# DLRM tower with a CIN: the first transfers in another order, a shorter tail of the program, and x_pair read from two copies

## The reference, cut to what matters

```python
e = jnp.stack([tbl_f[ids[:, f]] for f in range(32)], axis=1)      # 512 x 32 x 16
x0 = h = e
for i in range(3):                                                # W_i: 128 x (32 * G), G = 32, 64, 64
    z = (x0[:, :, None, :] * h[:, None, :, :]).reshape(B, F * G, E)
    y = relu(einsum('oc,bce->boe', W_i, z) + b_i)                 # 128 channels
    x_keep, h = (y[:, :64], y[:, 64:]) if i < 2 else (y, y)
    xs.append(x_keep)
z = sum(concat(xs, axis=1), axis=2)                               # 512 x 256
h = concat([z, dense_ctx], axis=1)                                # 512 x 272
h = maximum(h @ W_top1 + b_top1, 0); h = maximum(h @ W_top2 + b_top2, 0); y = h @ W_top3
```

## Time and profile before

| | |
|---|---|
| median of 3 runs | 548.99 us (548.51 to 549.04) |
| the profiled execution's own time | 548.4 us |
| its span, first to last instruction | 546.6 us |
| mean granted TensorE clock | 0.978 of full |
| PE busy | 505.7 us, 93% |
| DVE, ACT, POOL busy | 376.5, 198.8, 364.1 us |
| moved by DMA | 94.49 MB, mean 173 GB/s |

### The profile page before, as it was taken

The page is one execution under the profiler, slowest core; times in us unless marked ns, Lnnn a source line. Parts: engine busy times, 40 slices in busy tenths (PEclk is TensorE's granted clock), DMA queues, the critical chain, the costliest instruction groups (busy, mean ns, idle before and its releaser), DMA issues.

```text
span 546.6 us, 4327 instructions
## 1 busy us (share of the span) xinstructions
PE 505.7 (93%) x1474; PEld 277.4 (51%) x1474; DVE 376.5 (69%) x216; ACT 198.8 (36%) x257; POOL 364.1 (67%) x222
## 2 busy tenths in 40 slices
PE   0977947899999999999999999999999989899988
PEld 0733414455555555565555555555555554455555
DVE  1274526595959595959688695959595968967743
ACT  1212132433444443424342434434443525241244
POOL 5770527497969788796969696969697754715050
PEclk9988887899999999999999999999999999999999
DMA  7697989349997979797878787979789777451200
GB/s 229 144 201 204 210 221 196 100 98 252 222 251 170 255 159 254 158 227 166 230 164 226 172 215 165 225 167 244 164 197 222 171 190 161 90 110 11 74 0 0
DMA packets 33591, 94.49 MB, mean 173 GB/s; under 512 B 7889, under 2 KB 15057, under 8 KB 25122
## 3 DMA queue, kind: packets, MB, share of 16 engines
q1 hardware_dynamic: 27090, 90.82, 69.5%
q10 hardware_dynamic: 2384, 2.35, 2.0%
q0 software_dynamic: 4096, 1.06, 1.6%
HBM read 92.04 MB, written 2.10 MB: 172 GB/s over the span
## 4 chain that ended last, share of the span: by engine, by line
PE 73%; DMA 8%; DVE 7%; issue 4%; POOL 3%; SPq 2%; ACT 1%; POOLq 1%; DVEq 0%; ACTq 0%
PE acc L605 26%; PE acc L618 14%; PE spare L605 12%; PE x_bank L605 11%; DMA x_scratch<-gathered 4%; DVE z L414 4%; PE x_bank L618 3%; PE spare L618 3%; POOL gathered L349 3%; DMA gathered<-in_table,rows_all 2%; DMA x_rot<-x_scratch 1%; SPq L276 1%; POOLq L146 1%; DVE zl_parts L426 1%; PE acc L628 1%
## 5 line engine op out<-in xcount | busy, mean ns | idle before, releaser
L362 POOL TENSOR_TENSOR z_low<-z,z_high 128x1024 fp32r<-128x1024 f32 x90 | 221.4, 2472 | 130.1 <-ACT z_high L498 129.4
L414 DVE TENSOR_TENSOR z<-h,x_pair 128x2048 f32<-128x2048 f32 (+1 forms) x65 | 144.8, 2249 | 106.1 <-ACT h L512 104.6
L605 PE MATMUL acc<-z,w_direct 128*128 128x512 f32 x384 | 176.3, 603 | 15.2 <-DVE z L414 15.2
L349 POOL DMA_INDIRECT gathered<-in_table,rows_all x128 | 142.5, 1113 | 33.4 <-issue 27.1
L498 ACT ACTIVATE z_high<-z 128x1024 fp32r<-128x1024 f32 x90 | 93.3, 1054 | 145.1 <-DVE z L414 124.9
L605 PEld LDWEIGHTS acc<-z,w_direct 128*128 128x128 f32 x384 | 73.6, 193 | 95.7 <-issue 72.6
L605 PE MATMUL spare<-z,w_direct 128*128 128x512 f32 x200 | 92.4, 603 | 4.5 <-DVE z L414 4.5
L605 PE MATMUL x_bank<-z,w_direct 128*128 128x512 f32 x200 | 92.5, 608 | 3.9 <-DVE z L414 3.9
L414 DVE TENSOR_TENSOR z<-h_odd,x_pair 128x2048 f32<-128x2048 f32 x32 | 72.2, 2278 | 8.4 <-ACT h_odd L512 8.4
L414 DVE TENSOR_TENSOR z<-h_even,x_pair 128x2048 f32<-128x2048 f32 x32 | 72.2, 2279 | 7.9 <-ACT h_even L512 7.9
L605 PEld LDWEIGHTS spare<-z,w_direct 128*128 128x128 f32 x200 | 38.4, 193 | 47.9 <-issue 43.0
(11 more groups left out here) (140 smaller groups left out, 266.4 us busy)
## 6 DMA issues: line engine op xcount, KB each, us to landing
x_pair<-x_scratch SPq DMA_DIRECT2D x124, 512.0 KB, 7.3
x_rot<-x_scratch SPq DMA_DIRECT2D x60, 256.0 KB
x_rep<-x_scratch SPq DMA_DIRECT2D x15, 256.0 KB
w_direct<-in_W SPq DMA_DIRECT2D x2, 1024.0 KB, 8.5
gathered<-in_table,rows_all POOLq DMA_INDIRECT x128, 7.1
x_scratch<-gathered SPq DMA_DIRECT2D x32, 64.0 KB, 1.6
x_pair<-x_scratch ACTq DMA_DIRECT2D x4, 512.0 KB, 16.5
x_pair<-in_W_top SPq DMA_DIRECT2D x2, 512.0 KB, 4.7
```

What stands on the lines that cost most here:

```text
L349: pool.indirect_dma_start(gathered[:, c % X_SLOTS, j, :], None, table, bass.IndirectOffsetOnAxis(ap=rows.bitcast(U32), axis=0),).then_inc( ...
L362: nc.gpsimd.tensor_tensor(z_low[:, slot_of(pair)], products_of(pair), z_high[:, slot_of(pair)].bitcast(F32), ALU.subtract).then_inc(low_po ...
L414: nc.vector.tensor_tensor(z[:, step.group % Z_SLOTS, first:end], h[:].unsqueeze(1).to_broadcast([P, end - first, N]), x_pair[:, chunk % 2, ...
L605: op = nc.tensor.matmul(bank_of(pair)[:], w_direct[:, first + i], products_of(pair)[:, i], start=i == 0 and pair is OPENS[pair.layer, pair ...
```

## The change: what it does

- BUSY is 28 instead of 56.
- The x_pair loads of chunk 0: parts 0 and 1 from both queues, then the store of chunk 1, then parts 2 and 3 from SP. After that x0 of chunk 1, the store of chunk 2, parts 0 and 1 of chunk 1, then a wait for the product (0, 1, 0) and the squares of chunk 1, x0 of chunk 2, parts 2 and 3 of chunk 1. The loop leaves out what was moved.
- FIRST has (2, 0, 1) ahead of (0, 1, 0), and the split pairs of (0, 1) are due one step behind their product, not two. The product of (2, 0, 0) is made in two halves, as that of (1, 0, 0) was, with a signal after each.
- The split pairs of layer 2, chunk 15 get their low part from VectorE, one step after the product (LOWS).
- Top layers: the bias of the first one is a 17th row of the dense weights against a column of ones (K = 51); ACT makes the rounded ReLU in one pass; VectorE takes max(bank, 0) less the rounded part; the second layer's matmuls with the high part wait for ACT alone.
- load_half: of the 64 partitions of a half, even ones read the first copy of the rows in x_scratch and odd ones the second, 32 rows further on.

The diff, cut to its core (declarations, the host's arrays and renamed sizes are left out):

```diff
+DENSE = EMBED + 1
...
-BUSY = 56
+BUSY = 28
...
-FIRST = ([(1, 0, k) for k in range(GROUPS)] + [(2, 0, 0), (0, 1, 0)] + [(2, 0, k) for k in range(1, GROUPS)]
+FIRST = ([(1, 0, k) for k in range(GROUPS)] + [(2, 0, 0), (2, 0, 1), (0, 1, 0), (2, 0, 2), (2, 0, 3)]
          + [(1, 1, 0), (0, 2, 0)] + [(1, 1, k) for k in range(1, GROUPS)])
...
 def hands(layer, chunk, k):
-    return tuple("pool" if chunk and (layer, k, i) in AT else "tensor" for i in range(2))
+    low = "vector" if (layer, chunk) == (2, CHUNKS - 1) else "pool"
+    return tuple(low if chunk and (layer, k, i) in AT else "tensor" for i in range(2))
...
         for pair in step.by("vector", "pool"):
-            due[min(n + 2, len(PLAN) - 1)].append(pair)
+            due[min(n + (1 if (pair.layer, pair.chunk) == (0, 1) else 2), len(PLAN) - 1)].append(pair)
     return due
...
-BEHIND = behind()
+def lows():
+
+    due = {n: [] for n in range(len(PLAN))}
+    for n, step in enumerate(PLAN):
+        for pair in step.by("vector"):
+            due[min(n + 1, len(PLAN) - 1)].append(pair)
+    return due
+
+
+BEHIND, LOWS = behind(), lows()
+
+HALVED = (STEPS[1, 0, 0], STEPS[2, 0, 0])
...
         def load_half(eng, c, k, a):
-            rows = x_dram[c, ROT * a + GROUP * k:ROT * a + GROUP * (k + 1), :]
+
+            x = x_dram[c]
+            rows = bass.AP(x.tensor, x.offset + (ROT * a + GROUP * k) * N, [[0, HALF // 2], [FIELDS * N, 2], [1, GROUP * N]])
             eng.dma_start(x_pair[HALF * a:HALF * (a + 1), c % 2, GROUP * k:GROUP * (k + 1), :],
-                          rows.unsqueeze(0).to_broadcast([HALF, GROUP, N])).then_inc(xp_here[c % 2][k], 16)
+                          rows).then_inc(xp_here[c % 2][k], 16)
...
             store_x(sp, 0)
             sp.wait_ge(x_stored[0], 32)
-            for k in range(GROUPS):
+            for k in range(2):
                 load_half(sp, 0, k, 0)
             store_x(sp, 1)
+            for k in range(2, GROUPS):
+                load_pair(0, k)
             sp.wait_ge(start_done, 1)
             load_x0(sp, 1)
-            for k in range(GROUPS):
+            store_x(sp, 2)
+            for k in range(2):
                 load_pair(1, k)
+            wait_made(sp, STEPS[0, 1, 0])
+            sp.wait_ge(last_made, 2)
+            load_x0(sp, 2)
+            for k in range(2, GROUPS):
+                load_pair(1, k)
 
             for step in PLAN:
-                if step.layer == 1 and step.k == 0 and step.chunk + 2 < CHUNKS:
+                if step.layer == 1 and step.k == 0 and 1 <= step.chunk < CHUNKS - 2:
                     store_x(sp, step.chunk + 2)
-                if step.layer == 0 and step.chunk + 1 < CHUNKS:
+                if step.layer == 0 and 2 <= step.chunk < CHUNKS - 1:
                     wait_made(sp, step)
                     sp.wait_ge(last_made, step.chunk + 1)
                     load_x0(sp, step.chunk + 1)
...
 
             wait_made(sp, STEPS[1, CHUNKS - 1, GROUPS - 1])
             wait_made(sp, STEPS[2, CHUNKS - 2, GROUPS - 1])
-            tops = [(wd[EMBED * i:EMBED * (i + 1)], w_top1[2 * P:, :]) for i in range(COPIES)] + [
-                (wt1, w_top1[0:2 * P, :].rearrange("(k p) n -> p k n", p=P)),
+            tops = [(wd[DENSE * i:DENSE * (i + 1)], w_dense) for i in range(COPIES)] + [
+                (wt1, w_top1.rearrange("(k p) n -> p k n", p=P)),
...
-                runs = ((0, 2), (2, 4)) if step is PLAN[0] else ((0, 4),)
+                runs = ((0, 2), (2, 4)) if step in HALVED else ((0, 4),)
...
-                for pair in BEHIND[n]:
-                    if pair.by == "vector":
-                        low_part(pair)
+                for pair in LOWS[n]:
+                    low_part(pair)
...
-                split_top(hid1_rounded, m + 1, hid1[:, m, :], hid1_high[:, m, :], hid1_low[:, m, :], hid1_ready)
+                dve.wait_ge(hid1_rounded, m + 1)
+                nc.vector.scalar_tensor_tensor(out=hid1_low[:, m, :], in0=top_bank[m][:], scalar=0.0,
+                                               in1=hid1_high[:, m, :].bitcast(F32), op0=ALU.max,
+                                               op1=ALU.subtract).then_inc(hid1_ready, 1)
...
             act.wait_ge(x_stored[0], 32)
-            for k in range(GROUPS):
+            for k in range(2):
                 load_half(act, 0, k, 1)
...
                 act.wait_ge(top1_done, m + 1)
-                nc.scalar.activation(hid1[:, m, :], top_bank[m][:], ACT.Relu,
-                                     bias=bt1[:, m:m + 1]).then_inc(hid1_made, 1)
-                act.wait_ge(hid1_made, m + 1)
-                nc.scalar.activation(hid1_high[:, m, :], hid1[:, m, :], ACT.Copy).then_inc(hid1_rounded, 1)
+                nc.scalar.activation(hid1_high[:, m, :], top_bank[m][:], ACT.Relu).then_inc(hid1_rounded, 1)
...
-                if step is PLAN[0] and pair.i == 0:
-                    pe.wait_ge(first_made, 1)
+                if step in HALVED and pair.i == 0:
+                    pe.wait_ge(first_made, HALVED.index(step) + 1)
...
             pe.wait_ge(top_split, 4)
             for k in range(4):
+                pe.wait_ge(hid1_rounded, k + 1)
+                for m in range(2):
+                    cols = slice(k * 2 * P + m * P, k * 2 * P + (m + 1) * P)
+                    nc.tensor.matmul(acc[m][:], wt2_high[:, cols], hid1_high[:, k, :], start=k == 0, stop=False)
+                    nc.tensor.matmul(acc[m][:], wt2_low[:, cols], hid1_high[:, k, :], start=False, stop=False)
                 pe.wait_ge(hid1_ready, k + 1)
                 for m in range(2):
-                    first = k * 2 * P + m * P
-                    op = three_products(acc[m], (wt2_high, wt2_low), slice(first, first + P),
-                                        (hid1_high[:, k, :], hid1_low[:, k, :]), k == 0, k == 3)
+                    cols = slice(k * 2 * P + m * P, k * 2 * P + (m + 1) * P)
+                    op = nc.tensor.matmul(acc[m][:], wt2_high[:, cols], hid1_low[:, k, :], start=False, stop=k == 3)
                     if k == 3:
```

More of the change, by code:

```diff
@@ L142, in flat, with dlrm_tower @@
     return tiles.rearrange("p t o -> p (t o)")
-def dlrm_tower(nc, idx_in, row0_in, ident_in, sel_in, signs_in, columns_in, table, dense, w0_in, w12_in, w_top1, w_top2, out):
+def dlrm_tower(nc, idx_in, row0_in, ident_in, sel_in, signs_in, columns_in, table, dense, w0_in, w12_in, w_dense, w_top1, w_top2, out):
     with ExitStack() as ctx:
@@ L181, in dlrm_tower @@
         wl_parts = sb("wl_parts", [P, P], F32R)
-        columns = sb("columns", [P, 11])
-        bias, bt1, bt2, wt3 = columns[:, 0:3], columns[:, 3:7], columns[:, 7:9], columns[:, 9:11]
+        columns = sb("columns", [P, 7])
+        bias, bt2, wt3 = columns[:, 0:3], columns[:, 3:5], columns[:, 5:7]
         kept01 = sb("kept01", [P, 2, N])
@@ L189, in dlrm_tower @@
         sum2 = sb("sum2", [P, BATCH])
[L191 to L193 removed]
+        dense_rows = sb("dense_rows", [P, BATCH // P, COPIES, DENSE])
+        dense_high = sb("dense_high", [COPIES * DENSE, BATCH], F32R)
+        dense_parts = sb("dense_parts", [COPIES * DENSE, BATCH], F32R)
         result = sb("result", [1, BATCH])
[L196 to L197 removed]
+        wd_high = sb("wd_high", [COPIES * DENSE, N], F32R)
+        wd_parts = sb("wd_parts", [COPIES * DENSE, N], F32R)
         w0 = z[:, 2].rearrange("p t n -> p (t n)")[:, 0:(2 * GROUP + 1) * P].rearrange("p (t o) -> p t o", o=P)
@@ L211, in dlrm_tower @@
         wt2 = flat(x_pair[:, 0, 8:10, :])
-        wd = x_pair[0:COPIES * EMBED, 0, 10, :]
+        wd = x_pair[0:COPIES * DENSE, 0, 10, :]
         wt1_high, wt1_low = z_high[:, PAIR_SLOTS - 1], z_low[:, PAIR_SLOTS - 1]
@@ L435, in _ @@
             nc.vector.scalar_tensor_tensor(
-                out=dense_parts[:], in0=dense_high[:].bitcast(F32), scalar=signs[0:COPIES * EMBED, 2:3],
-                in1=dense_bank[0:COPIES * EMBED, :], op0=ALU.mult, op1=ALU.add).then_inc(dense_ready, 1)
+                out=dense_parts[:], in0=dense_high[:].bitcast(F32), scalar=signs[0:COPIES * DENSE, 2:3],
+                in1=dense_bank[0:COPIES * DENSE, :], op0=ALU.mult, op1=ALU.add).then_inc(dense_ready, 1)
             dve.wait_ge(first_copied, 1)
@@ L543, in _ @@
             act.wait_ge(dense_turned, 1)
-            nc.scalar.activation(dense_high[:], dense_bank[0:COPIES * EMBED, :], ACT.Copy).then_inc(dense_rounded, 1)
+            nc.scalar.activation(dense_high[:], dense_bank[0:COPIES * DENSE, :], ACT.Copy).then_inc(dense_rounded, 1)
             act.wait_ge(x_stored[0], 32)
-            for k in range(GROUPS):
+            for k in range(2):
                 load_half(act, 0, k, 1)
@@ L710 @@
     signs[2::GROUP, 1] = -1.0
-    signs[2 * EMBED:COPIES * EMBED, 2] = -1.0
-    signs[1 * EMBED:2 * EMBED, 3] = -1.0
+    signs[2 * DENSE:COPIES * DENSE, 2] = -1.0
+    signs[1 * DENSE:2 * DENSE, 3] = -1.0
     arrays = {
@@ L719 @@
         "table": np.concatenate(tables, axis=0),
[L720 removed]
```

(12 more changed lines are left out.)

9 lines of the change are left out of this document (3 added, 6 removed).

## The result

The changed kernel takes 544.41 us in the median of 12 runs, the kernel before 548.02 in 12 runs beside it: a ratio of 0.9942, 95% interval 0.9924 to 0.996, so 3.2 us less (2.2 to 4.2). Forecast were 539.6 us, 9.4 less, and a range of 536.0 to 542.5. The sign was right, and two thirds of the gain did not come.

A forecast was written before the change was run, and what follows sets the result against it. TensorE's matmuls were taken to bound the middle at 29.13 us a chunk, so only the two ends could gain: 9.2 (start) + 0.0 (last chunk) + 0.2 (top layers) = 9.4 us, from 548.99 to 539.6 us, range 536 to 542.5.

The forecast's parts named there:

- first transfers: Chunk 0's x_pair loads: parts 2 and 3 land at 37.5 and 42.3 us, cutting the 3.9 us shift to 0.6.
- x0 of chunk 2: Its early load removes VectorE's 7.83 us wait; TensorE's 11.0 us wait becomes 3.7, gaining 7.3 less 0.4 for the clock.
- Fewer transposes: At the start, 28 fewer at 142 ns each let the first layer-1 product start 3.9 us earlier, at 29.2.
- Halving: Layer 2 of chunk 0: matmuls start after half a product, 1.15 us earlier, plus 0.5 us from the clock.
- The clock: TensorE's granted clock falls after long waits, costing 1.6 to 1.9 us after 2.1 to 3 us, 2.9 after 3.9.
- the tail: Last chunk: VectorE's low parts swap the 1.55 us wait for POOL for a new 1.95 us wait; nothing gained.
- the two copies: x_pair loads reading two copies stay at 224 GB/s, so the edit gives 0 us.
- Top layers: At the end, one ACT pass and the bias in a matmul remove only a 0.2 us wait.
- B: Rival: clock falls at new waits, in the tail (+1.9) or chunk 0's x_pair stalls (+1.7); 541.5 us, both 543.2; chance 0.19.
- A: Rival: the two copies lift the x_pair load rate, 3.2 us less, 536.4 us; chance 0.13.
- C: Rival: slower two-copy reads make DMA the bound in the middle, 564 us at 170 GB/s; chance 0.04.
- D: Rival: chunk 2's store waits for late gathers, so its x0 stays late, 546 us; chance 0.05.

The follow-up runs named there:

- e6: The changed kernel with SP issuing x_pair parts 2 and 3 of chunk 0 ahead of the store of chunk 1: 540.11 us, ratio to before 0.9853.
- e0: The changed kernel run again with no edit, as a base: 544.67 us, ratio to before 0.9926.
- e3: The changed kernel with all four x_pair parts of chunk 0 sent first, from both queues, then the store of chunk 1: 538.44 us, ratio 0.9818.
- e4: The changed kernel with the last chunk's layer-2 low parts back on POOL: 544.94 us, ratio to before 0.9951.
- e10: e3 with 56 transposes instead of 28: 541.87 us, ratio to before 0.9884.
- e11: e3 with the product (2,0,0) made whole instead of in halves: 541.20 us, ratio to before 0.988.
- e15: e3 with 14 transposes instead of 28: 543.87 us, ratio to before 0.9904.
- e8: e3 with product (1,1,1) ahead of (0,2,0), whose split pairs are due one step behind: 538.67 us, ratio to before 0.9824.
- e12: e3 with x_pair read from one copy instead of two: 539.42 us, ratio to before 0.9831.
- e13: e3 run again unchanged, as a base on one chip: 539.08 us, ratio to before 0.9832.
- e14: e3 with the 64 partitions of a half reading 32 different sources, same bytes and instructions: 538.92 us, one run, no ratio.
- e5: The kernel before with only load_half changed, to read the two copies: 549.18 us, ratio to before 1.001.
- e2: The changed kernel with 56 transposes instead of 28: 545.85 us, ratio to before 0.9948.
- e1: The changed kernel with x_pair read from one copy instead of two: 543.93 us, ratio to before 0.9915.

## Why the prediction was wrong

**The step that failed: first transfers.** Its mechanism was right: SP waits for chunk 1's gathers and the parts come later than before. The size was not. Forecast were a release at 30.5, loads issued from 31.4, and 4.7 us a part: 37.5 and 42.3. The trace has the release at 31.6, loads issued from 32.5, a DMA share of 0.38 until 34, and landings at 41.5 and 47.1, so about 7.5 us for the first part from 34 and 5.6 for the second. The term that was mis-sized is the 4.7 us: I took the rate of a full queue, 224 GB/s, for a part on its own. The next part's loads and those of x_rep and x_rot stand on the queue behind it, and bytes of them seem to move in between, though the trace was not split by transfer: from 34 to 41.5 us the queues carried 1.5 MB (187 GB/s for 4 us, 213 for 3.5) for a part of 1.05 MB. Layer 1 of chunk 0 ended at 53.1 us, not 48.1: 5.0 of the 6.2 us that are missing between 9.4 and 3.2. With the wait taken out of the way (e6) the kernel takes 540.1 us, 0.9853 of the kernel before. That this is near the forecast (539.6 of 548.99, 0.983) is in part luck, as the forecast had this wait in it and had x0 of chunk 2 1.5 us too cheap.

The two profiles, followed from place to place, give the whole sum. TensorE's lead over the kernel before, with the forecast beside it:

| place | lead, us | forecast |
|---|---|---|
| start of layer 1, chunk 0 | 1.3 | 3.9 |
| its end | -4.4 | 0.6 |
| end of layer 2, chunk 0 | -2.5 | 2.3 |
| behind the wait for x0 of chunk 2 | 3.3 | 9.6 |
| in front of the 2.14 us wait | 2.0 | 9.2 |
| in the middle | 2.4 | 9.2 |

So halving and the new order of steps gave 1.9 us where 1.7 was forecast, and the low clock behind the 5.18 us wait cost 1.4 us and not 0.4.

**x0 of chunk 2: right mechanism, 1.5 us short.** VectorE's wait for x_rot went, and VectorE's own chain took its place, as the prediction said. The wait left is 5.18 us, not 3.7. The mis-sized term is the square part: 2.65 us instead of 0.75, while POOL's low part ran beside it:

```profile
76.43 3.24 POOL L384 TENSOR_TENSOR z_low<-z,z_high 128x1024 fp32r<-128x1024 f32 x1 [6.33 <-ACT z_high L522]
```

The forecast had put POOL's cost, 0.5 us, on the x0 product, which took 2.28 us. The same wait, 5.17 or 5.18 us, stands in e0, e3, e4, e6, e10, e11 and e15. In the changed kernel's trace the two square parts late in the run (at 431.99 and 463.04 us) also have a low part of POOL beside them and take 2.85 us; those that have none take 0.74, and so does the one that e8 moved away from it. The kernel before has the same two late ones, 2.86 us, so the price could have been read there. The Trainium skill ("SBUF — State Buffer", "Who interferes with whom") says that a VectorE instruction with two inputs in SBUF contends with POOL's reads; the trace agrees, 2.65 us beside POOL against 0.74 alone, and POOL's own low part took 3.24 us there, where such a part takes 2.4 us in the middle of the run.

**Fewer transposes: 3.9 us forecast, 1.3 in the trace, lost anyway.** Two terms were off: the average of 142 ns is that of 56, and the first 28 took 4.55 us, since the early ones are slower; and the clock fell in layer 0 of chunk 0, whose 8 records took 5.40 us for 3.70. The second is no loss in the sum: in the kernel before, the same fall came behind the 2.83 us wait (32 records in 15.67 us for 14.1), and in the changed kernel the 16 records there took 7.11 us, full speed. Nor does it come from having 28: e3, e12, e13 and e14 have 3.70 us with 28 transposes, and e5 has 5.81 with 56. That what is saved here is mostly lost in the wait for the parts was forecast, and e2 and e10 bear it out.

**Halving**: at least 1.1 us, as forecast for the wait. e11 measures 3.4 us against e3, or 2.6 against e3's second ratio (e13), and only 1.1 of them are seen in the profile.

**The clock.** The forecast took it that the clock falls behind each wait over 2 us, as it did four times of four in the trace of before. In the changed kernel it did not fall behind the two waits of 2.83 us (16 records in 7.11 and 7.10 us) nor behind that of 2.14 (8 in 3.70), where before 8 took 5.40. So the length of the wait does not decide it alone; what does stays open.

**Right**: the middle did not move (a DMA share of 0.87 for 0.86); the tail swapped one wait for another, 1.75 us where 1.95 was forecast, without a fall of the clock; the two copies are worth nothing; the 2.14 us wait stayed. Top layers: the 0.2 us wait went, but 0.6 us before L714 came.

**The rivals.** B, the clock falling at the new waits, did happen in the first profile: behind the wait of 4.97 us 16 records took 9.29 us for 7.1, with the granted clock at 0.50 until 46 us (at most 0.2 us of it can be a wait for the product of the last part). In e0 the waits there were 0.8 and 1.6 us and it did not. A is ruled out by e1, e5 and e12, which compare one copy with two, C by the middle. D in its stated form did not occur: the store of chunk 2 was issued at 42 us. The range failed because its upper end held no bound for a late part: the prediction had the rows for a landing under backlog, 11.85 and 17.82 us, and priced the parts at the queue's best rate.

## What to carry to other kernels

A load put behind a wait costs more than the wait: here the queues ran dry before it and filled after it with everything that had been held back. Put long loads that need nothing ahead of short ones that wait for something, and price a landing from the landings of like transfers in that stretch and not from bytes by peak rate. When a wait of one engine is removed, add up the next engine's chain with the durations it has beside its neighbour, not alone; and a saving at the start is worth measuring only once nothing later in the start absorbs it: the same 28 transposes were worth 1.2 us in one order and about 3 in the other.

## What the runs showed of the hardware that was not expected

TensorE's first work in the program is slow although the granted clock reads 1.00. In the kernel before it does 16 records, nearly all transposes, from 14 to 17 us and 30 from 18 to 21, and the clock reads 1.00 in both. In e15 the stretch from 20 to 28 us reads so (columns as in the earlier trace rows):

```profile
20.00:24.00 4.00, 4.00 (x6) 1.67 (x5) 0.82 (x2) 1.77 (x4) 3.09 (x4) 1.00 1.00 219
24.00:28.00 4.00, 4.00 (x5) 1.17 (x4) 1.96 (x4) 1.31 (x5) 3.09 (x4) 1.00 0.97 214
```

The seventh column, the clock, is 1.00, and yet TensorE, busy all the time, shows 5 or 6 matmul records in 4 us, where 16 records take 7.03 us at full speed, 9 in 4 us. That is nearer the pace of 1.2 GHz than of 2.4. The changed kernel's own 8 records of 5.40 us are different (24 to 28 us): there the clock column reads 0.59. So in the start of a program the durations of the matmuls have to be read, and the clock column does not tell.
